# A decoder's last expert layer: its first 16 tiles among the last four groups, with a table of their own

## The chip, the cores and the metric

The kernel runs on one core of a Trainium2 chip. The time is device microseconds (us) of one execution, the median of several. The engines are PE (TensorE: matmuls and transposes), DVE (VectorE), ACT (ScalarE), POOL (GpSimd) and SP (SyncE, which only issues DMAs). Each runs its own instruction stream strictly in order and waits for others through semaphores.

## The reference

A two-layer decoder with residual layer norms works on 64 x 64 = 4096 tokens of width 128. Layer 0: retention-like attention, cross attention, and eight experts that are computed for all tokens. Layer 1: attention, cross attention (its context is `ctx_2048`), and a block that the change concerns, attention followed by a mixture of experts:

```python
x1 = _layernorm(x + attn_out, g1, be1)
gate_probs = softmax(x1 @ Wg + bg)
topk_p, topk_i = top_k(gate_probs, 2)                    # 2 of 8 experts
topk_p = topk_p / sum(topk_p)
comb = sum(one_hot(topk_i, 8) * topk_p[..., None], axis=-2)
h = gelu(einsum('bsd,edf->bsef', x1, W1) + b1)           # 128 -> 512
y = einsum('bsef,efd->bsed', h, W2) + b2                 # 512 -> 128
return _layernorm(x1 + einsum('bse,bsed->bsd', comb, y), g2, be2)
```

Then comes the outer residual layer norm. Each token needs two of the eight experts, so there are 8192 pairs of a token and an expert.

## The kernel before

**Groups and slots.** The tokens are cut into 16 groups of 256. There are four sets of buffers, the slots s = 0 to 3, and four passes n; group 4n + s of a pass runs in slot s. In the first half (streams 0 to 15) each group goes through layer 0, and in the second (streams 16 to 31, so "group 28" to "group 31" are the last four) through layer 1 as far as the ranks of its rows. A stream is a generator that yields the name of its next step; `in_turn` (L413) runs an engine through a table of pairs (stream, count), `ORDERS`. These tables are written out for each engine and stage (sp1, pe1, act1, dve1, pool1 for the groups; sp3 to dve3 for the expert tiles; sp4 to act4 for the end), and they alone set which step stands behind which.

**The end of a group.** PE's last steps are: reductions of the attention ("fr", "frt"), output projection ("fo"), transposes of x1 ("t4"), gate logits ("g", four matmuls at L2166, before which ACT copies x1 at L1213) and ranks ("rk", L2171). ACT takes the exponential of the gate's two best. DVE takes sum and layer norm ("n3"), the choice of two ("g"), weights ("gb", which also adds the group's counts to `base`, L1423) and the rows' places ("rk", last at L1707). Each of a group's 512 pairs gets a row in `rows_x`, a DRAM table of 38912 rows of 132 floats (x1, token row, other expert, two gates), in which expert e owns the rows from 4096 e on. POOL writes them with four indirect scatters of 128 rows each (step "sc", L1081). SP stores the group's states ("fq.1": x_last, L845; "x1": x1_last, L848), which the end of the kernel loads again.

**Blank rows.** An expert's last tile is not full, so `rows_x` must be cleared before. After `blank` is set (`s_blank`), SP issues four DMAs of 5016 KB each (L818) right after the first loads, ahead of all the rest of sp1. POOL waits for them in `fetch` (L1009) before its first gather, at the start of the second half. In the first half SP also stores x_mid (step "gb", L796) and expert outputs ("ye3", "ye7") and loads the next pass's transposed inputs ("u7", L760).

**Expert tiles.** A tile is 256 rows of one expert; 39 tiles are enough for any routing. After all 16 groups, PE counts the rows of each expert (L2181), waits for the places of the last pass in all slots, and DVE makes from the counts a table of 39 pairs, row address and weight address (L1720 to L1732). SP meanwhile waits for each slot's places and stores, issues the first weights (L868, `Q<-in_wm`), waits for the scatters of all slots, and issues the first row loads (L862, `XW<-rows_x`). The first two rounds (`FIXED = 2`, eight tiles) have addresses that are known beforehand, since tile k of them is the first of expert k; the others take theirs from the table. Then the tiles run in rounds over the four slots, tile 4j + s in slot s:

- PE: two transposes of the rows ("tx", L1808), eight matmuls up in four steps ("up", L2196), sixteen down ("dn", L2203)
- ACT: copy of the transposed rows (L1323), four Gelu (L1327)
- DVE: the gates and addresses of the rows ("tp", L1740 to L1748), add of the bias ("ty", L1753; the weights of a slot are loaded again only after it) and two multiplications with the gates (L1756)
- POOL: two indirect scatters into `y_rows` ("sc", L1091)

At the end all results are loaded, summed on PE, normed and stored.

## Time and profile before

| | |
|---|---|
| median of 3 runs | 1558.77 us (1558.26 to 1558.95) |
| the profiled execution | 1557.2 us, of which the span is 1555.4 us |
| mean granted clock of PE | 0.965 of full |
| busy: PE, DVE, ACT, POOL | 88%, 71%, 60%, 43% of the span |
| groups 30 and 31 end (last places matmul to its end) | about 1312 us |
| expert tiles on PE | 1322 to 1481 us |
| after them, to the end | 74 us |

Times in the trace are us from the start of the span. The page gives the span in 40 slices of 38.9 us, each digit being the busy share in tenths. A row of the timeline reads: start, duration, engine, line, operation with output and inputs, and in brackets the idle time before it and what released it. In the waits, a row gives engine and line, what it waited for, and total, number and longest. SPq rows are a DMA from its issue until it landed.

### The profile page before, as it was taken

The numbers are of one execution on the slowest core, as the hardware profiler recorded it, in microseconds if no ns is written. First come the engines' busy times: TensorE is split into PE (matmuls) and PEld (weight loads), VectorE is DVE, ScalarE is ACT, GpSimd is POOL, SyncE is SP. The second block draws the span as 40 slices with busy tenths as digits, with TensorE's granted clock in tenths as the row PEclk, the third lists the DMA queues.
The fourth block names the chain that finished last, engine by engine and source line by source line (L and its number), as shares of the span: only waits on it lengthen the run. The fifth ranks groups of instructions, "written<-read, shape, count | busy, mean of one in ns | idle before, by whom it ended". The sixth has DMA issues, their size and how long they took to land.

```text
span 1555.4 us, 47442 instructions
## 1 busy us (share of the span) xinstructions
PE 1366.5 (88%) x19262; PEld 1123.0 (72%) x19262; DVE 1109.8 (71%) x3476; ACT 935.6 (60%) x2469; POOL 671.9 (43%) x1048
## 2 busy tenths in 40 slices
PE   5899999999988998899998899998899984999951
PEld 4688888888876777676776677776777763888851
DVE  3777787887876758888667887778876775445556
ACT  2555665655544687855878658795568962545412
POOL 5514433533316214655234753337441344254455
PEclk8899999999999999999999999999999996999985
DMA  9952122121022000110000110011100003676851
GB/s 333 384 174 83 35 83 92 53 65 66 15 74 74 9 12 18 44 30 29 10 21 25 36 43 10 14 32 37 29 23 9 13 23 100 208 224 211 237 148 42
DMA packets 112155, 123.21 MB, mean 79 GB/s; under 512 B 21984, under 2 KB 85216, under 8 KB 111680
## 3 DMA queue, kind: packets, MB, share of 16 engines
q1 hardware_dynamic: 105344, 106.53, 21.7%
q0 software_dynamic: 6592, 13.64, 2.8%
q8 instruction: 152, 2.49, 0.7%
q14 instruction: 67, 0.55, 0.1%
HBM read 64.99 MB, written 55.15 MB: 77 GB/s over the span
## 4 chain that ended last, share of the span: by engine, by line
PE 48%; DVE 23%; POOL 8%; ACT 8%; issue 6%; DMA 5%; SPq 2%; DVEq 0%; POOLq 0%; ACTq 0%
PE bank L1949 6%; PE bank L1816 5%; PE bank L1801 3%; PE bank L1828 3%; DMA Q<-in_wm 2%; PE bank L2036 2%; PE bank L2071 2%; PE bank L1997 2%; DVE P L1581 2%; DVE gs L1580 2%; ACT P L1226 2%; PE bank L1993 2%; PE bank L2203 2%; PE bank L2196 2%; POOL rows_x L1081 2%
## 5 line engine op out<-in xcount | busy, mean ns | idle before, releaser
L1816 PE MATMUL bank<-const,P 128*128 128x128 f32 x1152 | 167.9, 280 | 9.9 <-ACT P L1226 4.1
L1816 PEld LDWEIGHTS bank<-const,P 128*128 128x128 f32 x1152 | 129.8, 142 | 39.4 <-ACT P L1226 10.0
L1226 ACT ACTIVATE P<-bank,gs 128x128 f32<-128x128 f32 x512 | 141.3, 393 | 26.4 <-DVE gs L1570 25.9
L1949 PE MATMUL bank<-XT,wb 128*128 128x256 f32 x512 | 140.4, 398 | 7.0 <-ACT PT L1131 3.8
L1036 POOL TENSOR_TENSOR P<-P,gs 128x512 f32<-128x512 f32 x64 | 66.5, 1047 | 157.1 <-DVE gs L1617 156.7
L1234 ACT ACTIVATE PT<-bank 128x512 f32<-128x512 f32 x192 | 108.2, 614 | 28.9 <-PE bank L1816 28.6
L1091 POOL DMA_INDIRECT y_rows<-R,gidx x78 | 74.7, 958 | 92.5 <-DVE R L1756 73.7
L1570 DVE TENSOR_REDUCE gs<-bank 128x4 f32<-128x512 f32 x128 | 82.1, 682 | 39.4 <-PE bank L2071 38.8
L1949 PEld LDWEIGHTS bank<-XT,wb 128*128 128x128 f32 x512 | 89.3, 192 | 22.2 <-ACT PT L1131 7.5
L1580 DVE TENSOR_REDUCE gs<-bank 128x8 f32<-128x512 f32 x128 | 87.1, 681 | 24.5 <-PE bank L2009 12.1
L1198 ACT ACTIVATE P<-bank 128x256 f32<-128x256 f32 x128 | 48.5, 380 | 84.5 <-PE bank L1949 83.8
L1327 ACT ACTIVATE PT<-bank,Q 128x256 f32<-128x256 f32 x156 | 64.8, 475 | 56.5 <-PE bank L2196 55.7
L946 POOL TENSOR_SCALAR rstd<-mv 128x2 f32<-128x2 f32 x80 | 18.1, 226 | 183.1 <-DVE mv L1358 182.3
L1219 ACT ACTIVATE P<-P 128x512 f32<-128x512 f32 x128 | 80.3, 643 | 19.7 <-DVE P L1581 19.3
L1581 DVE TENSOR_TENSOR P<-bank,gs 128x512 f32<-128x512 f32 x128 | 88.5, 691 | 4.4
L1081 POOL DMA_INDIRECT rows_x<-XW,places x64 | 64.4, 1006 | 49.4 <-DVE places L1707 39.3
L2196 PE MATMUL bank<-XT,Q 128*128 128x256 f32 x312 | 77.1, 385 | 4.8 <-DMA Q<-in_wm 4.8
L1828 PEld LDWEIGHTS bank<-wb,P 128*128 128x128 f32 x512 | 73.5, 193 | 9.7 <-DVE P L1511 4.6
L1828 PE MATMUL bank<-wb,P 128*128 128x128 f32 x512 | 78.4, 280 | 2.3 <-DVE P L1511 2.2
L1015 POOL DMA_INDIRECT Q<-y_mid,first_rows x64 | 64.3, 1004 | 29.5 <-DVE first_rows L1556 16.6
L2203 PE MATMUL bank<-Q,PT 128*128 128x128 f32 x624 | 76.1, 275 | 0.0
L2203 PEld LDWEIGHTS bank<-Q,PT 128*128 128x128 f32 x624 | 74.8, 192 | 1.5
(298 smaller groups left out, 3723.3 us busy)
## 6 DMA issues: line engine op xcount, KB each, us to landing
Q<-in_wm SPq DMA_DIRECT2D x39, 578.5 KB, 4.2
rows_x<-blank SPq DMA_DIRECT2D x4, 5016.0 KB, 37.7
y_mid<-PT SPq DMA_DIRECT2D x16, 512.0 KB, 3.1
y_mid<-D SPq DMA_DIRECT2D x16, 512.0 KB, 3.0
XW<-rows_x SPq DMA_DIRECT2D x39, 132.0 KB, 2.5
wb<-in_wb SPq DMA_DIRECT2D x1, 4228.0 KB, 15.0
V<-in_ctxT SPq DMA_DIRECT2D x32, 128.0 KB, 3.4
XT<-in_xT SPq DMA_DIRECT2D x16, 128.0 KB, 2.2
```

The source lines that it names most:

```text
L1081: pool.indirect_dma_start(d["rows_x"][:, :], bass.IndirectOffsetOnAxis(ap=places[:, (n * SLOTS + s) * T + t, k:k + 1], axis=0), XW[s][:, t ...
L1219: act.activation(P[s][:, i, :], P[s][:, i, :], ACT.Exp, scale=scale).then_inc(p.of(s), 1)
L1226: ins = act.activation(P[s][:, i, 128 * g:128 * g + 128], banks[s][i][:, 128 * g:128 * g + 128], ACT.Exp, bias=gs[s][:, 0, 4 * i + g:4 * i ...
L1234: act.activation(dst[:, i, :], banks[s][i][:, :], ACT.Copy).then_inc(pT.of(s), 1)
L1570: dve.tensor_reduce(gs[s][:, 0, 4 * i:4 * i + 4], banks[s][i][:, :].rearrange("p (g m) -> p g m", m=128), AX.X, ALU.min).then_inc(b_s_sub. ...
L1580: st2(dve.tensor_reduce(mx, v, AX.X, most))
L1581: dve.tensor_tensor(P[s][:, i, :].rearrange("p (g m) -> p g m", m=width), v, each(mx, width), ALU.subtract).then_inc(s_sub.of(s), 1)
L1816: last = pe.transpose(tile(banks[s][i], t), tile(P[s][:, i, :], t), ident)
L1828: last = mm(tile(half(s, i + 1), t), tile(P4[s][:, i + 1, :], t), tile(B("down"), e), start=True, stop=True)
L1949: mm(half(s, 2 * (e % 2) + k), tile(B("gu"), 2 * e + k), XT[s][:, :], start=True, stop=True).then_inc(a_up_ps.of(s), 1)
L2196: mm(half(s, c), tile(part(wm[s], WM, "w1"), c), XT[s][:, :], start=True, stop=True).then_inc(m_up_ps.of(s), 1)
L2203: ins = mm(tile(half(s, 0), t), tile(PT4[s][:, c, :], t), tile(part(wm[s], WM, "w2"), c), start=c == 0, stop=c == NC - 1)
```

## The change

- **Early tiles.** The tiles are split into 16 early ones and 23 late ones. The early tiles are full tiles: the table for them is made from the counts of the first 12 groups whose rows are ranked (`COUNTED`, `EARLY_PASSES = 3`), of which at least 16 tiles are complete. They sit in slots by `EARLY_SLOTS`: slot 0 has tiles 0, 1, 2, 4, 6, 9, slot 1 has 3, 5, 7, 10, 13, slot 2 has 8, 11, 14 and slot 3 has 12, 15. Their steps stand in the tables of the groups (sp1, pe1, act1, dve1, pool1), among the steps of groups 28 to 31.
- **Waits of a slot's first tile.** SP waits for the table and the last use of the group's buffers to load weights, and for the group's own stores and scatters of all four passes and the other slots' of three passes to load rows. PE waits for the slot's places.
- **Two tables.** PE takes the count inside "rk" of the 12th and of the 16th group ranked, DVE copies it to `plan`. `early_table` (stream 33) stands in dve1 right behind the end of group 27, `late_table` (stream 50) among the early tiles. The first four late tiles wait for the second table and all scatters; all 39 tiles take their addresses from the table.
- **Clearing.** The four DMAs at the start go. After each of the 16 x_mid stores ("gb") SP clears one of 16 parts, about 1.25 MB each; the first gather waits for all 16.
- **Orders.** All tables are new. In those of the groups common steps shift by at most 14 positions; in the last stage group 8 stands ahead of 5.

Near the end PE's order now reads (group in brackets, t0 is tile 0; several "fr", "fn", "fs" and "fp" steps left out): [29] rk, [31] fp1, [30] fr1, **[t0] tx**, [31] fp1, [30] frt, [30] fo, [31] fr1, **[t0] up, up.1, up.2**, [31] fn, **[t0] up.3**, [31] frt, fo, [30] t4, **[t3] tx**, [30] g, **[t0] dn, [t3] up, up.1**, [31] t4, [30] rk, **[t3] up.2, up.3**, [31] g, **[t1] tx, [t3] dn, [t5] tx, [t1] up, up.1, up.2**, [31] rk, **[t1] up.3, [t5] up**, and then only tiles, in the order 0, 3, 1, 5, 8, 2, 12, 7, 11, 4, 15, 10, 6, 14, 13, 9. ACT: [31] fp1, **[t0] tx**, [30] frt, [31] fp1.1, fr1, **[t0] up**, [31] frt, **[t0] up.1 to up.3**, [30] t4, **[t3] tx**, [30] g, **[t3] up, up.1**, [31] t4, **[t3] up.2, up.3**, [31] g. DVE: [31] n3, **[t0] ty**, [30] gb, rk, **[t3] tp**, [31] g, **[t3] ty**, [31] gb, rk. SP: [31] out1, fq.1, [29] fq.1, x1, [28] fq.1, x1, **[t0] tw, tx, [t3] tw, tx**, [30] fq.1, x1, **[t8] tw, [t1] tx, tw**, [31] x1, **[t5] tx, tw, [t8] tx**. POOL: [28] sc, [29] sc, fo and n3 of [30] and [31], **[t0] sc**, [30] sc, **[t3] sc**, [31] sc, **[t1] sc**.

```diff
-FIXED = 2
-ROUNDS = [(TILES - s + SLOTS - 1) // SLOTS for s in range(SLOTS)]
+EARLY_PASSES = 3
+EARLY_SLOTS = (0, 0, 0, 1, 0, 1, 0, 1, 2, 0, 1, 2, 3, 1, 2, 3)
+EARLY = len(EARLY_SLOTS)
+LATE = TILES - EARLY
+TILE_SLOTS = EARLY_SLOTS + tuple(k % SLOTS for k in range(LATE))
+ROUNDS = [TILE_SLOTS.count(s) for s in range(SLOTS)]
+COUNTED = (EARLY_PASSES * SLOTS, EARLY_PASSES * SLOTS + SLOTS)
+TURNS = [(i, TILE_SLOTS[:i].count(s), s) for i, s in enumerate(TILE_SLOTS)]
...
+            def clear_rows(k):
+                fours = XROWS // 128 // 4
+                lo, hi = fours * k // groups, fours * (k + 1) // groups
+                sp.dma_start(d["rows_x"].rearrange("(p a r) d -> p a (r d)", p=128, r=4)[:, lo:hi, :],
+                             over(blank[:, :], hi - lo)).then_inc(s_clear, 16)
...
+                if n == 0 and s == 0:
+                    sp.wait_ge(s_blank, 1)
+                clear_rows(n * SLOTS + s)
...
-            for at in range(0, each_row, BLANK):
-                sp.dma_start(d["rows_x"].rearrange("(p a r) d -> p a (r d)", p=128, r=4)[:, at // 4:(at + BLANK) // 4, :],
-                             over(blank[:, :], BLANK // 4)).then_inc(s_clear, 16)
...
-            for s in range(SLOTS):
-                sp.wait_ge(b_g_done.of(s), b_g_done.at(passes - 1, s))
-                sp.wait_ge(kept[s], 32 * passes)
-                load_weights(0, s)
-            for s in range(SLOTS):
-                sp.wait_ge(scattered[s], 16 * 2 * T * passes)
-            for s in range(SLOTS):
-                load_rows(0, s)
...
-            def tile(j, s):
-                yield "tx"
-                if j == FIXED:
-                    sp.wait_ge(s_table, 1)
+            def tile(i, j, s):
                 if j:
+                    yield "tx"
+                    if i - EARLY in range(SLOTS):
+                        sp.wait_ge(s_table, 2)
+                        for other in range(SLOTS):
+                            sp.wait_ge(scattered[other], 16 * 2 * T * passes)
                     sp.wait_ge(m_x_ps.of(s), m_x_ps.at(j - 1, s))
                     sp.wait_ge(m_row.of(s), m_row.at(j - 1, s))
-                    load_rows(j, s)
-                yield "tw"
-                if j:
+                    load_rows(i, s)
+                    yield "tw"
                     sp.wait_ge(m_y.of(s), m_y.at(j - 1, s))
-                    load_weights(j, s)
-                if 1 <= j <= 2:
-                    load_last_x1(j - 1, s)
-                    load_last_x(j - 1, s)
-
-            in_turn(sp, ORDERS["sp3"], [tile(j, s) for j in range(ROUNDS[0]) for s in range(SLOTS) if j < ROUNDS[s]])
+                    load_weights(i, s)
+                else:
+                    yield "tw"
+                    sp.wait_ge(s_table, 1)
+                    sp.wait_ge(b_s_ps.of(s), b_s_ps.at(passes - 1, s, use=7))
+                    load_weights(i, s)
+                    yield "tx"
+                    sp.wait_ge(kept[s], 32 * passes)
+                    for other in range(SLOTS):
+                        sp.wait_ge(scattered[other], 16 * 2 * T * EARLY_PASSES)
+                    sp.wait_ge(scattered[s], 16 * 2 * T * passes)
+                    load_rows(i, s)
+                if i >= EARLY and (i - EARLY) // SLOTS < 2:
+                    load_last_x1((i - EARLY) // SLOTS, s)
+                    load_last_x((i - EARLY) // SLOTS, s)
...
+                if emitted[n, s] + 1 in COUNTED:
+                    k = COUNTED.index(emitted[n, s] + 1)
+                    dve.tensor_copy(plan[0:1, NE * k:NE * k + NE], banks[s][1][0:1, T * NE:T * NE + NE]).then_inc(s_count, 1)
...
-            dve.tensor_copy(prim[:, :], prim[:, :]).then_inc(s_count, 1)
-            dve.wait_ge(s_count, 2)
...
+            def tiles_of(found, inner, at, n):
+
+                mid(dve.tensor_tensor(grid(S(at, 64), NE), grid(one(C("upto")), NE), over(found, NE), ALU.mult))
+                mid(dve.tensor_reduce(S(at + 64, NE), grid(S(at, 64), NE), AX.X, ALU.add))
+                mid(dve.tensor_tensor(grid(S(at + 72, 7 * n), 7), each(one(C("tile"))[:, 0:n], 7), over(S(at + 64, 7), n), ALU.is_ge))
+                mid(dve.tensor_tensor(grid(S(at + 240, 7 * n), 7), grid(S(at + 72, 7 * n), 7), over(inner, n), ALU.mult))
+                dve.tensor_reduce(S(at + 410, n), grid(S(at + 240, 7 * n), 7), AX.X, ALU.add)
+                mid(dve.tensor_reduce(S(at + 440, n), grid(S(at + 72, 7 * n), 7), AX.X, ALU.add))
+
+            def put_table(i0, at, n):
+                mid(dve.scalar_tensor_tensor(S(at + 500, n), S(at + 440, n), CAP / NT, S(at + 470, n), ALU.mult, ALU.add))
+                dve.tensor_scalar(grid(S(at + 530, 2 * n), 2)[:, :, 0], S(at + 500, n), float(NT), None, ALU.mult)
+                mid(dve.tensor_scalar(grid(S(at + 530, 2 * n), 2)[:, :, 1], S(at + 440, n), 128.0, None, ALU.mult))
+                dve.tensor_copy(table[:, i0:i0 + n, :], grid(S(at + 530, 2 * n), 2)).then_inc(s_table, 1)
+
+            full, done, step, left, inner = S(160, NE), S(168, NE), S(176, 7), S(184, NE), S(192, 7)
+
+            def early_table():
+                yield "pl"
+                at = 220
+                dve.wait_ge(s_count, 1)
+                mid(dve.tensor_tensor(grid(S(16, 128), 16), each(S(0, NE), 16), over(one(C("steps")), NE), ALU.is_ge))
+                mid(dve.tensor_reduce(full, grid(S(16, 128), 16), AX.X, ALU.add))
+                tiles_of(full, full[:, 0:7], at, EARLY)
+                mid(dve.scalar_tensor_tensor(S(at + 470, EARLY), S(at + 410, EARLY), -1.0, one(C("tile"))[:, 0:EARLY], ALU.mult, ALU.add))
+                put_table(0, at, EARLY)
+                yield "pl.1"
+                mid(dve.tensor_scalar(S(144, NE), S(at + 64, NE), float(EARLY), None, ALU.min))
+                dve.tensor_copy(done[:, 0:1], S(144, 1))
+                mid(dve.tensor_tensor(done[:, 1:NE], S(145, 7), S(144, 7), ALU.subtract))
+                mid(dve.tensor_tensor(step, done[:, 1:NE], done[:, 0:7], ALU.subtract))
+
+            def late_table():
+                yield "pl"
+                at = 220
+                dve.wait_ge(s_count, 2)
+                mid(dve.tensor_tensor(grid(S(16, 128), 16), each(S(NE, NE), 16), over(one(C("below")), NE), ALU.is_gt))
+                mid(dve.tensor_reduce(left, grid(S(16, 128), 16), AX.X, ALU.add))
+                mid(dve.tensor_tensor(left, left, done, ALU.subtract))
+                mid(dve.tensor_tensor(inner, step, left[:, 0:7], ALU.subtract))
+                tiles_of(left, inner, at, LATE)
+                mid(dve.tensor_tensor(S(at + 470, LATE), S(at + 410, LATE), one(C("tile"))[:, 0:LATE], ALU.add))
+                mid(dve.tensor_scalar(S(at + 470, LATE), S(at + 470, LATE), done[:, 0:1], None, ALU.add))
+                put_table(EARLY, at, LATE)
...
+                if emitted[n, s] + 1 in COUNTED:
+                    mm(banks[s][1][0:1, T * NE:T * NE + NE], C("full")[:, 0:1], base[:, emitted[n, s] + 1, 0, :], start=True, stop=True)
...
-            pe.wait_ge(s_count, 1)
-            for s in range(SLOTS):
-                pe.wait_ge(b_g_done.of(s), b_g_done.at(passes - 1, s))
-            mm(banks[0][0][0:1, 0:NE], C("full")[:, 0:1], base[:, groups, 0, :], start=True, stop=True).then_inc(s_count, 1)
-            pe.wait_ge(s_table, 1)
-
-            def tile_of(j, s):
+            def tile_of(i, j, s):
                 yield "tx"
                 pe.wait_ge(tile_x[s], 16 * (j + 1))
                 if j:
                     pe.wait_ge(m_y.of(s), m_y.at(j - 1, s))
+                else:
+                    pe.wait_ge(b_g_done.of(s), b_g_done.at(passes - 1, s))
```

## Rows read from the trace of the kernel before

**Rows 1.** Page, part 2: PE busy tenths and moved GB/s in 40 slices.

```profile
PE   5899999999988998899998899998899984999951
...
GB/s 333 384 174 83 35 83 92 53 65 66 15 74 74 9 12 18 44 30 29 10 21 25 36 43 10 14 32 37 29 23 9 13 23 100 208 224 211 237 148 42
```

**Rows 2.** Stretches: length, busy (count) PE PEld DVE ACT POOL, clock, DMA, GB/s; page part 5.

```profile
1295.00:1313.30 18.30, 6.73 (x30) 5.04 (x28) 10.54 (x62) 1.56 (x5) 8.71 (x12) 0.60 0.39 134
...
1313.30:1322.30 9.00, 0.20 (x2) 0.13 (x3) 3.81 (x16) 0.00 (x0) 3.83 (x4) 0.50 0.45 131
...
1322.30:1481.30 159.00, 150.54 (x1014) 137.76 (x1014) 76.75 (x426) 76.96 (x196) 71.13 (x75) 0.99 0.73 220
...
L2196 PE MATMUL bank<-XT,Q 128*128 128x256 f32 x312 | 77.1, 385 | 4.8 <-DMA Q<-in_wm 4.8
```

**Rows 3.** Timeline, end of last groups: start, us, engine, line, operation [idle before <-releaser].

```profile
1300.78 1.02 PE L2166 MATMUL bank<-wb,XT 128*128 128x8 f32 x4 [0.47 <-ACT XT L1213]
...
1307.47 1.08 POOL L1081 DMA_INDIRECT rows_x<-XW,places  x1 [4.08 <-DVE places L1707]
...
1311.64 0.58 PE L2171 MATMUL bank<-gs,const 128*128 128x16 f32 x2 [3.32 <-DVE base L1423]
...
1322.31 0.66 PE L1808 MATMUL bank<-const,XW 128*128 128x128 f32 x2 [8.45 <-DMA XW<-rows_x]
```

**Rows 4.** Waits from 1322 to 1482: us in total, times, longest.

```profile
PE bank L1808 <- DMA XW<-rows_x: 12.0, 7, 8.5
...
PE bank L2196 <- DMA Q<-in_wm: 4.8, 6, 1.2
...
DVE small L1740 <- DMA Q<-in_wm: 24.5, 13, 6.4
```

**Rows 5.** Timeline of POOL: first scatter of group 28 and of group 29.

```profile
1255.58 1.08 POOL L1081 DMA_INDIRECT rows_x<-XW,places  x1 [9.97 <-DVE places L1707]
...
1286.84 1.08 POOL L1081 DMA_INDIRECT rows_x<-XW,places  x1 [10.04 <-DVE places L1707]
```

**Rows 6.** DMA issues (times, KB, median us to landing), and landing of line 868.

```profile
XW<-rows_x SPq DMA_DIRECT2D x39, 132.0 KB, 2.5
...
rows_x<-XW,places POOLq DMA_INDIRECT x64, 2.4
...
DMA to landing us min/median/max: 3.5/4.2/6.6
```

**Rows 7.** Timeline of ACT: first Gelu of the tile stage.

```profile
1324.43 0.66 ACT L1323 ACTIVATE XT<-bank 128x256 f32<-128x256 f32 x2 [1.05 <-PE bank L1808]
...
1325.11 1.28 ACT L1327 ACT_TABLE_LOAD   x1
```

**Rows 8.** Timeline of DVE (table), and line 1753 over the run: ns min/median/max.

```profile
1313.89 0.28 DVE L1720 TENSOR_TENSOR plan<-bank,const 1x128 f32<-1x128 f32 x1 [0.31 <-PE bank L2181]
...
1317.56 0.24 DVE L1732 CAST table<-plan 1x78 int32<-1x78 f32 x1
...
L1753 DVE TENSOR_TENSOR R<-bank,Q x39: 423/424/426, 1330.6 to 1481.3; 128x256 f32<-128x256 f32 x39
```

**Rows 9.** Timeline of PE, the same operations at other times.

```profile
1267.27 0.61 PE L2166 MATMUL bank<-wb,XT 128*128 128x8 f32 x4
...
1324.19 1.83 PE L2196 MATMUL bank<-XT,Q 128*128 128x256 f32 x4
...
1330.45 1.03 PE L2196 MATMUL bank<-XT,Q 128*128 128x256 f32 x4
```

**Rows 10.** Stretches, as rows 2.

```profile
1120.00:1160.00 40.00, 38.29 (x582) 30.04 (x581) 32.76 (x91) 26.89 (x68) 17.34 (x29) 1.00 0.09 25
```

**Rows 11.** Last blank DMA, a PE wait between 40 and 460, first gather.

```profile
50.09 14.14 SPq L818 DMA_DIRECT2D rows_x<-blank  x1
...
PE bank L1841 <- DMA XT<-in_xT: 2.1, 1, 2.1
...
464.31 1.22 POOL L1015 DMA_INDIRECT Q<-y_mid,first_rows  x1 [16.64 <-DVE first_rows L1556]
```

More of the change, by code:

```diff
@@ L62 @@
                       ("cos", 64), ("sin", 64), ("par", 2), ("side", 2), ("quad", 4), ("iota", 8),
-                      ("ones", 8), ("full", 128), ("before", 128), ("eoff", 8), ("steps", 16), ("upto", 64),
+                      ("ones", 8), ("full", 128), ("before", 128), ("eoff", 8), ("steps", 16), ("below", 16), ("upto", 64),
                       ("tile", TILES), ("rowbase", 32), ("spare", TILES * T))
@@ L1757, in tile @@
                 ins.then_inc(m_gated.of(s), 1)
-            in_turn(dve, ORDERS["dve3"], [tile(j, s) for j in range(ROUNDS[0]) for s in range(SLOTS) if j < ROUNDS[s]])
+            in_turn(dve, ORDERS["dve1"], [whole(n, s, first, second) for n in range(passes) for s in range(SLOTS)]
+                    + [whole(n, s, first2, second2) for n in range(passes) for s in range(SLOTS)]
+                    + [between(), early_table()] + [tile(*turn) for turn in TURNS[:EARLY]] + [late_table()])
+            in_turn(dve, ORDERS["dve3"], [tile(*turn) for turn in TURNS[EARLY:]])
             def finish(n, s):
```

118 lines of the change are left out of this document (53 added, 65 removed), and 446 rows, old and new, of tables (ORDERS, act1, act3, dve1).

## The prediction

> **What bounds the kernel now.** I read the page's slices first [rows 1]: of the 40 slices, TensorE is busy eight tenths or more in all but the first (5), the 34th (4) and the last two (5 and 1). So time is lost where its row dips, and the dip in the 34th is where the change works. The table of stretches [rows 2] prices it. From 1295.0 to 1313.3, while groups 30 and 31 (the last two) end, PE is busy 6.73 of 18.3 us; from there to 1322.3 it is busy 0.20 of 9.0; then all 39 expert tiles run in 159.0 us with PE busy 150.54. The timeline [rows 3] says why. Gate logits of group 30 are at 1300.78, its scatter starts at 1307.47, the place matmuls of group 31 are at 1311.64: short steps handed between PE, ACT and DVE with nothing else queued. Then PE counts the rows, DVE makes the table, POOL scatters, SP loads tile rows, and PE gets them at 1322.31. In the waits [rows 4] this load is the one long one (8.5 us); the tile stage has otherwise waits of at most 1.2 us, so it is bound by PE.
>
> **The unit.** One tile is 150.54 / 39 = 3.86 us of PE. By the page its eight up matmuls, four steps of two, take 77.1 / 39 = 1.98 [rows 2], 0.5 a step ("up"); of the rest I give 0.4 to the transposes ("tx") and 1.5 to the sixteen down matmuls ("dn").
>
> **Part 1: sixteen tiles enter before the old end.** Read from the decoded orders, few of them truly run among the groups: between "fr1" of group 30 and "rk" of group 31 PE now does tile 0 and tile 3 whole, tx of tiles 1 and 5 and three of the four up steps of tile 1: 2 x 3.86 + 2 x 0.4 + 3 x 0.5 = 10.0 us. The PE holes of 1295 to 1313 (11.6 us) are about that large. Are the rows there? Tile 0 (slot 0) needs group 28's scatter, which began at 1255.58 and, four issues of 1.3 us and 2.4 us of landing later, is in by 1264; tile 3 (slot 1) needs group 29's, begun at 1286.84, in by 1294.3, plus a 2.5 us load: 1297 [rows 5, 6]. Both are in time. SP's new order puts "fq.1" of group 31 ahead of the final stores of groups 29 and 28; in the trace such a store waits for its data anyway, until about 1273, which is still 15 us early.
>
> The other fourteen early tiles (all but 0 and 3) follow group 31's "rk" with no wait for the count, the table or all scatters; those are due only for tile 16, some 50 us later. So the 9.0 us hole and the rest of it goes. What is late next is slot 2's row load (scatter of group 30, issued from 1307.47 [rows 3], now behind tile 0's y scatter of 2 x 1.26 us on POOL): landed about 1317, loaded 1319.5, while PE has tiles 1 and 5 to do until about 1319. Slot 3's load lands about 1326, PE comes to it at 1327. Neither costs over 1 us.
>
> **Part 2: what the insertion delays.** The chain of groups 30 and 31 sets where the rest starts.
> - ACT must switch between Gelu (tiles) and Exp (the gates, "g"). The order has Gelu, Exp for group 30, Gelu, Exp for group 31, Gelu: four switches more than before. A load took 1.28 us [rows 7]. Two stand in the chain: +2.6 us. The Trainium skill (ScalarE: Activation LUTs, What ACT_TABLE_LOAD costs) speaks against this mixing: it states 1283 ns for the load plus some 1380 ns of drain at every switch. The trace agrees with the first number and shows no drain: the copy before ended within 0.03 us of the load. By the page the chain would be 2.8 us longer, and the forecast 1549.
> - DVE takes "ty" of tiles 0 and 3 ahead of "gb" of group 30 and of group 31: 0.42 us for the add [rows 8] and about as much for the two gate steps, +1.8 us if both are waited for.
> - Against it, a PE that has work keeps its clock. The granted clock was 0.60 of full in the mean from 1295 to 1313 and 0.50, the 1.2 GHz level, from there to 1322, while PE idled; the logits took 1.02 us there and 0.61 at 1267.27, before the fall [rows 2, 3, 9]. I take -1.5 us over both groups.
> Net +3: between -1.5 (all hidden) and +7 (all in series, plus up steps ahead of the logits). So rk of group 31 ends at 1315.6 instead of 1312.6.
>
> **Part 3: the rest of the tiles.** Remaining PE work: 150.5 - 10.0 - 1.3 (the cold start: the first four up matmuls took 1.83 us, four later ones 1.03, and so the transposes and the steps after them, some 0.5 more [rows 9]) = 139.2 us. Idle of the tile stage was 159.0 - 150.54 = 8.5 us. It grows where a slot is used again too soon: weights wait for "ty", so y add 0.42, issue 0.35, landing 4.2 [rows 6, 8] and about 0.5 for signals, 5.5 us, must lie under other tiles' PE work. The old order left three tiles (11.6 us) between two of one slot. The new one has four places with one tile between (3.9 us: stall 1.6 each) and about six with two (7.7 us: covered unless the landing is the slowest, 6.6). Two of the four are inside the group chain where PE waits anyway. I add 4 us, bounds 0 and 12. End of tile work: 1315.6 + 139.2 + 12.5 = 1467.3 against 1481.3: **14.0 us earlier**.
>
> **Part 4: table and count.** The old table, 13 DVE steps from 1313.89 to 1317.80, lay inside the hole that goes. Now the early table, some 20 small DVE steps, stands after group 27's ranks, near 1127. At the price of the old one, 13 steps in 3.9 us [rows 8], it is 4 to 6 us of DVE in one piece, where DVE is busy 32.76 of 40 us and PE 38.29 [rows 10]. Four groups are in flight and cover most; I take 1 us of PE, bounds 0 and 5. The late table is under tiles where DVE is busy half the time [rows 2]: nothing; without that cover it would be 5 us. The two added count matmuls replace one, before the place matmuls of two groups: nothing.
>
> **Part 5: clearing.** The same 20 MB go out in 16 pieces of 1.25 MB, each behind an x_mid store, instead of four at 18 us that hold SP's queue until 64 us and move 333 and 384 GB/s in the first two slices, 174 in the third [rows 1, 11]. What waited behind them on SP were loads for the next round; PE waited for such a load once in the first stage, 2.1 us [rows 11]. Gain at most 2.1. Cost: at 384 GB/s a piece is 3.3 us of all engines, ahead of y stores and xT loads on SP, 16 times, 0 to 4 us in all. At the hand-over near 451 to 464 the last piece lands by about 460, before first_rows is ready at 464.31 [rows 11]; with that cover gone each late us would count. I take 0, bounds -2 and +4.
>
> **Part 6: new orders elsewhere.** Positions shift by at most 14 among some 1200 to 2150 steps; in the tail, 74.1 us from 1481.3 to the end, the reduction of group 8 moves ahead of 5. No row prices them: 0, bounds -4 and +4, some two times the 1.7 us that PE idles in a 40 us window [rows 10].
>
> **Sum.** The profiled execution has a span of 1555.4 us and took 1557.2, 1.8 outside the span and 1.6 under the median 1558.77. Change: -14.0 + 1 = -13.0, taken from the median: **1546 us**.
>
> **Rivals.**
> - *Only the hole goes.* If inserted tiles push groups 30 and 31 back by as much as they take, the gain is 1312.6 to 1322.3, 9.7, plus 1.3 cold start, less 4 and 1: 6 us, 1553. For it: PE, ACT and DVE run strictly in order and there are four table loads. Against it: PE's holes there are real waits.
> - *Everything fits.* No delay of the chain, no reuse stalls: 3 + 4 more, and 1 or 2 from the clearing: 1538.
> - *Nothing left.* The price of reuse or of the phase orders eats it: 1556 to 1562.
> - *Slower: slots starve.* Slot 0 has six of the sixteen tiles, slot 1 five. SP's single queue holds a weight load behind another slot's row load, which waits for PE. If each of the ten short reuses costs 4 us, 40 instead of 4: +36 - 13.0, 1582; it decides from 2 us each (20 against 4 + 13.0). For it: landings up to 6.6 us [rows 6], and DVE waited for them 13 times, 24.5 us in all, with four slots in turn [rows 4]. Against it: those PE waits were at most 1.2 us [rows 4].
>
> **How the numbers follow.** Forecast 1540 to 1551: 0.52. Everything fits: 0.12, a third of it under 1536. Only the hole: 0.17. Nothing left, within 0.2% (3.1 us, about what a measurement can tell from no change): 0.10. Slower: 0.09. Faster by over 0.2% is the first three: 0.81. The range 1536 to 1557 leaves out 0.04 below and about 0.15 above.
>
> **What would show it.** Right: PE busy some 9 or 10 us more between 1290 and 1316; no PE wait of 8.5 us for rows_x; a clock near 1.0 through 1300 to 1340; five or so ACT table loads near 1300; the last dn near 1467 and a tail of the same 74 us. Wrong: the stretch of groups 30 and 31 longer by as much as its tiles take; PE waits for Q<-in_wm of over 2 us each; PE idle near 1130 or at 451 to 480 grown by several us, which would put the time above 1551.

## The result, and the profile after

The changed kernel takes 1550.84 us (median; 1542.93 to 1556.62), the kernel before in the same comparison 1558.16 (1554.7 to 1559.53): a ratio of 0.9953, 95% interval 0.9937 to 0.9968, or 7.3 us faster. The forecast was 1546, range 1536 to 1557. The number lies in the range, and the sign is right. The mechanism behind it is not: the experiments below show that merging tiles and groups, as this change does it, brings nothing that can be measured, and that the two new sets of orders alone reach the same time, which I had put at 0. That the number held is luck.

The profiled execution of the changed kernel took 1556.62 us, the longest of its executions, with a span of 1554.8. So its total says little, but its stages can be compared with those of other traces. From its page, part 2 (busy tenths of PE, its clock and GB/s moved, 40 slices), which answers to [rows 1]:

```profile
PE   6799999999989998899998899998999987898871
...
PEclk9999999999999999999999999999999999999986
...
GB/s 255 10 160 153 73 134 136 115 136 94 53 160 54 16 9 25 40 26 28 10 28 18 47 33 9 14 32 35 31 23 9 9 25 107 189 227 222 200 186 42
```

The dip of the 34th slice is gone (4 before, 7 now); so are the 333 and 384 GB/s of blank rows in the first two slices, now spread over the first twelve. But slices 35 to 38 read 8988 where they read 9999 before. What was filled was opened again.

To see where time goes, I cut the span at events that both kernels have: the first gather on POOL (start of the second half), the end of the place matmuls of groups 19, 27 and 31, the end of the last down matmul, and the end. The table of stretches at these cuts, first of before, then of after (length; busy and count of PE, PEld, DVE, ACT, POOL; clock, DMA share, GB/s):

```profile
0.00:464.30 464.30, 423.92 (x4733) 364.13 (x4734) 346.30 (x1071) 256.76 (x677) 179.58 (x272) 0.97 0.36 122
464.30:718.90 254.60, 231.82 (x3850) 182.16 (x3849) 191.60 (x519) 169.88 (x444) 119.29 (x188) 0.99 0.11 31
718.90:1125.60 406.70, 374.18 (x6679) 291.96 (x6679) 317.53 (x878) 290.42 (x771) 190.38 (x303) 1.00 0.09 26
1125.60:1312.60 187.00, 159.24 (x2892) 125.21 (x2891) 131.68 (x373) 127.69 (x349) 67.23 (x107) 0.95 0.09 28
1312.60:1481.30 168.70, 150.79 (x1017) 137.89 (x1016) 81.10 (x444) 76.96 (x196) 74.96 (x79) 0.96 0.71 214
1481.30:1555.40 74.10, 26.57 (x96) 21.63 (x96) 41.53 (x195) 13.92 (x32) 40.42 (x100) 0.69 0.31 90
```

```profile
0.00:460.90 460.90, 422.19 (x4733) 362.23 (x4734) 348.27 (x1070) 255.40 (x678) 179.78 (x273) 0.99 0.35 123
460.90:714.10 253.20, 232.55 (x3849) 182.12 (x3847) 193.43 (x519) 168.97 (x443) 119.72 (x188) 0.98 0.11 31
714.10:1129.40 415.30, 379.77 (x6682) 296.91 (x6682) 322.74 (x878) 291.26 (x771) 190.36 (x303) 0.99 0.09 25
1129.40:1322.20 192.80, 173.17 (x2958) 135.80 (x2958) 139.22 (x412) 139.16 (x368) 71.14 (x111) 0.96 0.12 36
1322.20:1485.10 162.90, 145.04 (x953) 130.02 (x952) 75.89 (x425) 70.95 (x182) 71.75 (x76) 0.98 0.70 212
1485.10:1554.80 69.70, 24.70 (x96) 20.02 (x96) 41.23 (x195) 14.04 (x32) 40.59 (x100) 0.73 0.32 95
```

Three things are to be seen. The fifth row: 953 matmul instructions instead of 1017 stand behind group 31's ranks, so about 2.4 tiles were done before, as meant; yet the stretch is only 5.8 us shorter, and the one before it 5.8 us longer. In these two traces the merging nets zero. The third row: groups 20 to 27, in which no tile runs, are 8.6 us longer with the same instructions. The first and last row: 3.4 and 4.4 us shorter. I had put the three together at 0, plus or minus 4.

The same cuts in every trace of this study (us; the last column is the ratio to the kernel before of the same comparison, with its interval):

| kernel | to first gather | to 19 | 20 to 27 | 28 to 31 | tiles | end | ratio |
|---|---|---|---|---|---|---|---|
| before | 464.3 | 254.6 | 406.7 | 187.0 | 168.7 | 74.1 | 1 |
| before, again (b0) | 464.0 | 254.1 | 406.6 | 188.4 | 169.7 | 73.5 | |
| after | 460.9 | 253.2 | 415.3 | 192.8 | 162.9 | 69.7 | 0.9953 (0.9937 to 0.9968) |
| a0 (after, again) | 457.4 | 253.6 | 412.5 | 193.5 | 164.1 | 69.7 | 0.9961 (0.9945 to 0.9976) |
| clear_at_start | 459.0 | 252.8 | 414.0 | 191.1 | 163.0 | 69.8 | 0.9929 (0.9913 to 0.9946) |
| tiles_behind | 458.2 | 254.5 | 412.1 | 185.4 | 175.0 | 69.8 | 1.0001 (0.9986 to 1.0016) |
| old_tail | 461.4 | 254.0 | 412.6 | 190.3 | 164.7 | 73.5 | 0.9986 (0.9969 to 1.0004) |
| round_robin | 457.1 | 253.0 | 414.7 | 190.4 | 155.2 | 71.5 | 0.994 (0.9923 to 0.9957) |
| old_second_half | 459.1 | 255.1 | 405.5 | 199.8 | 163.9 | 69.0 | 0.995 (0.9933 to 0.9968) |
| exp_tiles | 458.2 | 254.6 | 416.3 | 192.9 | 165.8 | 70.0 | 0.9973 (0.9958 to 0.9987) |
| ty_between | 457.4 | 253.1 | 413.0 | 189.8 | 163.4 | 69.8 | 0.9957 (0.994 to 0.9973) |
| middle_old | 456.1 | 254.0 | 406.2 | 193.7 | 164.3 | 69.1 | 0.9907 (0.9889 to 0.9926) |
| no_merge | 462.1 | 254.8 | 412.3 | 185.1 | 172.2 | 70.6 | 0.9951 (0.9933 to 0.9968) |
| best | 457.7 | 253.0 | 406.5 | 193.3 | 152.9 | 70.7 | 0.9891 (0.9871 to 0.991) |

A trace is one execution, the ratio many. I read a stage only where several traces agree, and take the verdict from the ratio. A stage's length also moves with the granted clock of its execution, so for the tiles I read the idle time of PE (length less busy), with the mean clock beside it. It is 17.9 us in before (0.96), 17.9 in after (0.98), 18.6 in a0 (0.98), and 17.2 to 20.8 in all eight traces that have the changed kernel's slots with tiles among the groups; 14.0 in round_robin (1.00) and 9.6 in best (0.98).

### The profile page after: what moved, and what is told of

Same layout as the page of the kernel before. It is cut to its first block, busy times and chain, and to the rows that moved or that the text cites. A ratio compares the mean times of both kernels' runs of the same rounds, so it can differ in the third digit from the quotient of the medians.

```text
span 1554.8 us, 47583 instructions
## 1 busy us (share of the span) xinstructions
PE 1377.4 (89%) x19264; PEld 1127.1 (72%) x19264; DVE 1120.8 (72%) x3497; ACT 939.8 (60%) x2473; POOL 673.3 (43%) x1048
## 4 chain that ended last, share of the span: by engine, by line
PE 44%; DVE 25%; POOL 10%; ACT 8%; issue 6%; DMA 5%; SPq 2%; DVEq 0%; POOLq 0%; ACTq 0%
PE bank L1856 5%; PE bank L1989 4%; PE bank L2111 2%; PE bank L1868 2%; PE bank L2076 2%; PE bank L1841 2%; PE bank L2037 2%; PE bank L2238 2%; PE bank L2033 2%; DVE gs L1588 2%; DVE P L1589 2%; POOL rows_x L1088 2%; PE bank L2231 2%; DMA Q<-in_wm 2%; POOL rstd L954 2%
## 5 line engine op out<-in xcount | busy, mean ns | idle before, releaser
L1856 PE MATMUL bank<-const,P 128*128 128x128 f32 x1152 | 169.6, 283 | 10.9 <-ACT P L1226 4.0
L1241 ACT ACTIVATE PT<-bank 128x512 f32<-128x512 f32 x192 | 109.3, 619 | 33.5 <-PE bank L1856 33.4
L953 POOL TENSOR_SCALAR rstd<-mv 128x2 f32<-128x2 f32 x80 | 18.2, 228 | 191.6 <-DVE mv L1365 190.4
L1226 ACT ACTIVATE P<-P 128x512 f32<-128x512 f32 x128 | 80.1, 642 | 18.6 <-DVE P L1589 18.0
L1088 POOL DMA_INDIRECT rows_x<-XW,places x64 | 64.2, 1003 | 31.9 <-DVE places L1718 20.8
```

Of the source, the lines that this page charges most:

```text
L1088: pool.indirect_dma_start(d["rows_x"][:, :], bass.IndirectOffsetOnAxis(ap=places[:, (n * SLOTS + s) * T + t, k:k + 1], axis=0), XW[s][:, t ...
L1226: act.activation(P[s][:, i, :], P[s][:, i, :], ACT.Exp, scale=scale).then_inc(p.of(s), 1)
L1241: act.activation(dst[:, i, :], banks[s][i][:, :], ACT.Copy).then_inc(pT.of(s), 1)
L1856: last = pe.transpose(tile(banks[s][i], t), tile(P[s][:, i, :], t), ident)
```

## Is the spread the kernel's own? a0 and b0

```diff
 (a0: the changed kernel; b0: the kernel before; no edit)
```

> The changed kernel as it is, in the same call as the next three, so that they can be compared with it. Its executions so far lay between 1543 and 1557 us. If that spread belongs to the kernel, these lie in the same band, median near 1550, and execution time falls as the mean granted clock rises (0.970 at 1554, 0.979 at 1541). If it came from the chip of the first job, they lie within 3 us of each other.

> The kernel before once more, for a second trace. If the stages differ between the kernels and not between executions, it shows first gather near 464, 406 to 408 us from the ranks of group 19 to 27, 187 to 31, 169 to the last down matmul and 74 to the end, each within 1.5 us.

a0: 1552.59 us (1549.08 to 1554.69), ratio 0.9961 against before. b0: 1558.27 us, and each stage within 1.5 us of the first trace, as expected. So 6 to 10 us more in groups 20 to 27 and 2 to 5 us less at the end are the kernel's and not chance: all traces with the respective order show them. To the first gather all traces with the new order are shorter too, by 2 to 8 us, but only 2 to 3 us of it can be put down to the order: where the mean clock of that stage is as low as in before (0.97), in old_tail and no_merge, it takes 461.4 and 462.1 us against 464.0 and 464.3. The changed kernel spreads by 14 us in the first comparison and by 6 in this; in both the time falls as the granted clock rises (correlation -0.83 and -0.77).

## What the orders alone bring: no_merge

```diff
 (the kernel before; FIXED, table, count, clearing and the tile stage untouched)
-ORDERS sp1, pool1, act1, dve1, pe1: of before
+ORDERS sp1, pool1, act1, dve1, pe1: of after, steps of tiles and tables left out
-ORDERS sp4, pool4, act4, dve4, pe4: of before
+ORDERS sp4, pool4, act4, dve4, pe4: of after
```

> The kernel before with nothing of the change but its orders: of the groups (tile steps left out) and of the last stage. Tiles, table, count and clearing are as before. My forecast put 14 us of gain into the merging of tiles and groups and nothing into the orders: then this equals the kernel before. The stage table says the reverse: first gather 5 us sooner, end 4 us shorter, groups 20 to 27 7 us longer, groups 28 to 31 2 us shorter, the tile stage as before (169 us), together 1553 to 1555, which is nearly all of the change's gain.

1552.53 us (1548.18 to 1559.07), ratio 0.9951 (0.9933 to 0.9968). The whole change has 0.9953 and 0.9961. So all that was done to the tiles, the two tables and the clearing, adds nothing that can be measured (each interval reaches some 2.5 us either way) to what two sets of orders bring. The reason of the forecast is refuted though its number held. The trace of this run is of its slowest execution (1559.07), so its stages don't add up to the gain; the stage differences that several traces share (about -2 to -5 to the first gather, +7, -2, -4 at the end) sum to -1 to -4 us; the rest of the 7.6 isn't located.

## Does merging bring what it was to bring? tiles_behind and round_robin

**tiles_behind** puts the early tiles behind the groups again, in their new sequence of slots:

```diff
+def behind(order, first, keep=()):
+    pairs = list(zip(order[0::2], order[1::2]))
+    late = [p for p in pairs if p[0] >= first and p[0] not in keep]
+    return sum([p for p in pairs if p not in late] + late, ())
+for _name, _first, _keep in (("sp1", 32, (32, 35)), ("pool1", 32, ()), ("act1", 32, ()), ("dve1", 34, ()), ("pe1", 33, ())):
+    ORDERS[_name] = behind(ORDERS[_name], _first, _keep)
```

> The changed kernel with every early tile step of PE, ACT, DVE and POOL behind the last step of group 31 (SP keeps the loads of the first two slots where they are). If the inserted tiles fill true holes of groups 30 and 31 and delay them by 3 us, as forecast, 10 us of PE work now follow instead: 6 to 8 us slower than the changed kernel. If only the hole between the stages brings the gain (the inserted tiles push the groups back by what they take), it is the same within 2 us, and group 31's places are ranked near 1312 instead of 1322.

1558.15 us, ratio 1.0001: 5.6 us slower than a0, near the 6 to 8 of the first theory and far from "the same". The stages show both halves of the forecast's Part 1 and 2: without the inserted tiles groups 28 to 31 take 185.4 us (185.1 in no_merge) instead of 190.3 to 193.5, so 9 to 10 us of tile work cost the groups 5 to 8. That is more than the 3 I took. And the tile stage, with no hole for count and table any more, takes 175.0 us, more than the 168.7 with that hole; 2.0 us of this are idle time (19.9 against 17.9), 4.3 are busy time of the same work. PE's waits from 1310.2 to 1485.2 (line, releaser: us in total, times, longest):

```profile
PE bank L2241 <- DMA Q<-in_wm: 10.3, 13, 1.8
PE bank L1858 <- DMA XW<-rows_x: 6.3, 6, 2.2
```

Before it was 4.8 for the weights and 12.0 for rows, of which 8.5 was the hole [rows 4]. Without it, 8.3 us of waiting for loads have become 16.6. In the changed kernel itself, from 1285 to 1482:

```profile
PE bank L2231 <- DMA Q<-in_wm: 10.4, 11, 2.0
PE bank L1848 <- DMA XW<-rows_x: 6.0, 5, 2.8
```

None is longer than 2.8 us, so no single stall stands out on a timeline. The hole has gone and many small waits have taken its place. The suspect is the slots, six of 16 tiles in slot 0 and five in slot 1. Counted in the tables of PE, 3 of the 35 times that a slot comes again it does so with one other tile between, and 12 times with two; in the kernel before it is 0 and 7, with three or more between in the rest.

**round_robin** tests that. Slots in turn give 2 and 7 such places; the order of the tiles and the place of the second table change with them:

```diff
-EARLY_SLOTS = (0, 0, 0, 1, 0, 1, 0, 1, 2, 0, 1, 2, 3, 1, 2, 3)
+EARLY_SLOTS = (0, 1) + (0, 1, 2, 3) * 3 + (0, 1)
-TILE_SLOTS = EARLY_SLOTS + tuple(k % SLOTS for k in range(LATE))
+TILE_SLOTS = EARLY_SLOTS + tuple((k + 2) % SLOTS for k in range(LATE))
-ORDERS: tiles 0, 3, 1, 5 (slots 0, 1, 0, 1) among the groups, then 8, 2, 12, 7, 11, 4, ...
+ORDERS: tiles 0, 1, 2, 3 (slots 0, 1, 0, 1) at the same places, then 4, 5, ... in the relative order of before
```

> The changed kernel with two tiles instead of tile 0 and tile 3 at their places among the groups, and all later tiles in turn over the four slots in the relative order of the kernel before. In the first comparison the stretch from the last ranks to the last down matmul holds 163 to 165 us, of which some 22 are idle, 16 of them waits for weights and rows. If slots that come again too soon cause that, the stretch falls to 150 to 155 us and the time by 8 to 12 us against the changed kernel. If something else fills it (the stores of the groups, scatters, the clock), it stays within 3 us.

1548.06 us (1543.71 to 1553.52), ratio 0.994. The stretch of the tiles is 155.2 us against 162.9 and 164.1, at the edge of what was expected. In the table of stretches:

```profile
1315.20:1470.40 155.20, 141.22 (x953) 127.75 (x952) 77.17 (x425) 71.12 (x183) 70.17 (x74) 1.00 0.72 220
```

Of these 7.7 us, 3.9 are the slots': idle time of PE is 14.0 us where the changed kernel has 17.9. The other 3.8 are busy time, 141.2 instead of 145.0 for the same 953 instructions, with a clock of 1.00 instead of 0.98, and so belong to this execution, the fastest of its kernel (1543.71). Of the whole time 2 to 4.5 us show against the changed kernel, less than the 8 to 12 expected and with intervals that overlap (0.9923 to 0.9957, and 0.9945 to 0.9976 for a0); 1.7 us go at the end, where PE waited 10.3 us instead of 8.6 for the results to be loaded. That the slots cause idle time is shown by PE's waits for weights and rows (11.8 us here, 15.3 to 19.2 in the traces with the changed slots); the whole time alone doesn't settle it.

## The insertion among the groups: exp_tiles and ty_between

**exp_tiles** has the exponential in place of Gelu in the tiles, so it leaves that layer's function out and ACT needs no other table:

```diff
-                    act.activation(PT4[s][:, c, :], half(s, c), ACT.Gelu, bias=...)
+                    act.activation(PT4[s][:, c, :], half(s, c), ACT.Exp, bias=...)
```

> The changed kernel with exponential instead of Gelu in the last layer's tiles, which leaves the function of that layer out, so that ACT needs no other table among the groups. If the four added loads of 1.28 us lie in the chain of the last two groups as forecast (two of them), the ranks of group 31 come 2 to 5 us sooner after those of group 29, and the time is 2 to 4 us lower. If PE has other work meanwhile, the time is the same within 1.5 us.

1553.35 us, ratio 0.9973; no table load between 1290 and 1345, and 34.2 us from the ranks of group 29 to those of 31, the same as in the changed kernel (34.2 and 36.2). The mean clock of that stretch was 0.90 in exp_tiles and in the first trace of the changed kernel, both 34.2 us, so these two can be compared: the loads cost nothing that shows. The timeline of ACT in the changed kernel shows why:

```profile
1307.02 0.38 ACT L1327 ACTIVATE XT<-bank 128x256 f32<-128x256 f32 x1
1307.42 1.28 ACT L1322 ACT_TABLE_LOAD   x1
1309.12 0.20 ACT L1322 ACTIVATE small<-small 128x2 f32<-128x2 f32 x1 [0.42 <-DVE small L1396]
...
1315.24 1.28 ACT L1322 ACT_TABLE_LOAD   x1
1316.76 0.20 ACT L1322 ACTIVATE small<-small 128x2 f32<-128x2 f32 x1 [0.24 <-DVE small L1396]
```

Both loads for the gates' exponential are done while DVE still chooses the two experts: the exponential waits 0.42 and 0.24 us for DVE after them. In exp_tiles the first of these waits is 1.72 us, about the load and the wait together. The copy ended 0.02 us before the load began. The Trainium skill (ScalarE: Activation LUTs, What ACT_TABLE_LOAD costs) counts a drain of some 1380 ns beside the load; no switch here shows it. The ratio's interval (0.9958 to 0.9987) overlaps that of a0 (0.9945 to 0.9976), so this is no difference, and in any case not the 2 to 4 us of gain.

**ty_between** takes away the other suspect. The timeline of DVE in the changed kernel, with the steps of group 31's gate, tile 3's bias add ("ty") and group 31's "gb":

```profile
1316.33 0.39 DVE L1395 CAST gs<-gidx 128x4 f32<-128x4 uint32 x1
1316.41 0.31 DVE L1396 TENSOR_TENSOR small<-gs 128x2 f32<-128x2 f32 x1
1318.99 0.42 DVE L1790 TENSOR_TENSOR R<-bank,Q 128x256 f32<-128x256 f32 x1 [2.27 <-PE bank L2238]
1319.85 0.16 DVE L1419 TENSOR_SCALAR XW<-const 128x2 f32<-128x2 f32 x1
```

The exponential was ready at 1316.96; DVE held "gb" back until 1319.85, for the down matmuls of tile 3 and its add: 2.9 us, of which I had counted 0.9 as work and nothing as a wait for PE. But most of that wait is the clock. PE's down matmuls of tile 0 and of tile 3 in the same trace:

```profile
1307.64 2.03 PE L2238 MATMUL bank<-Q,PT 128*128 128x128 f32 x16
...
1315.27 3.68 PE L2238 MATMUL bank<-Q,PT 128*128 128x128 f32 x16 [0.31 <-ACT PT L1331]
```

From 1315.4 to 1318.8 the granted clock was 0.50. Where the lower level missed tile 3 (old_tail, exp_tiles), its sixteen took 2.05 us and DVE waited 0.65 us; where it fell on them (after, a0, clear_at_start, round_robin), 3.56 to 3.74 us, and DVE waited 2.16 to 2.80.

```diff
 (dve1 only)
-[31] n3, [t0] ty, [30] gb, rk, [t3] tp, [31] g, [t3] ty, [31] gb, rk
+[31] n3, [30] gb, [t0] ty, [30] rk, [t3] tp, [31] g, [31] gb, [t3] ty, [31] rk
```

> The changed kernel, but on DVE the bias add and gate steps of tile 0 and of tile 3 stand behind gb of groups 30 and 31 instead of ahead of it (ahead of rk). In a trace of the changed order DVE sat idle 2.7 us before the add of tile 3 until PE's sixteen down matmuls ended, with gb of group 31 ready behind it. If this wait is what delays the last two groups, their ranks come 2 to 4 us sooner after those of group 29 (36.2 and 34.2 us in two traces) and the time is 2 to 4 us lower. If the ranks wait for PE's own work ahead of them, the same within 1.5 us.

Its trace has 33.1 us from the ranks of group 29 to those of 31. That is no proof of a gain: with the chain unedited clear_at_start has 33.4 and old_tail 32.5 us (mean clock 0.95), round_robin and after 34.0 and 34.2 (0.90, as in ty_between), a0 36.2 (0.81). At the same clock it is 1 us less. The time is 1552.69 us, ratio 0.9957, not to be told from 0.9961. A miss, and PE's timeline of the changed kernel shows why. Between tile 3's down matmuls and group 31's ranks stand steps of tiles 5 and 1:

```profile
1319.57 0.41 PE L1848 MATMUL bank<-const,XW 128*128 128x128 f32 x2 [0.61 <-DVE R L1790]
1319.81 1.46 PE L2231 MATMUL bank<-XT,Q 128*128 128x256 f32 x6
1321.47 0.20 PE L2212 MATMUL bank<-base,const 128*1 128x8 f32 x2 [0.20 <-DVE base L1431]
```

The first of them itself waits for tile 3's add (0.61 us). PE came to the ranks only 0.20 us before DVE's "gb" was ready (0.21 in a0, round_robin and clear_at_start). The expectation's second branch holds: the ranks wait for PE's own work ahead of them. From the ranks of group 29 to those of 31 PE is busy 26.57 us in after and 15.68 in before; 10.9 us more of work lengthen the stretch by 5.1.

## The orders of the groups and of the end

**old_second_half** and **middle_old** go back to the old order of the groups (PE, ACT, DVE, POOL), the first from the end of group 19 on, the second only to the end of group 27. At these cuts old and new order have done exactly the same steps.

```diff
 (middle_old; counts are steps)
-pe1 1152 to 1860, act1 811 to 1295, dve1 667 to 1057, pool1 221 to 389: order of after
+pe1 1152 to 1860, act1 811 to 1295, dve1 667 to 1057, pool1 221 to 389: order of before
```

> The changed kernel with the order of the groups as before from the end of group 19 on (PE, ACT, DVE, POOL; SP's stays new), tile steps behind the same group steps. From the ranks of group 19 to those of group 27 the trace of before took 406.7 us and five traces with the new order 412.1 to 415.3. If the new order of these groups costs that, 4 to 6 us faster than the changed kernel. My term for it was 0, plus or minus 4; if the difference is chance of single executions, the same within 2 us.

> The changed kernel with the order of the kernel before on PE, ACT, DVE and POOL from the end of group 19 to the end of group 27 only, and the new order up to there and from there. That stretch took 405.5 us with the old order in the kernel with the old second half, 406.7 and 406.6 in two traces of before, and 412 to 416 with the new. If it is the order, 6 to 8 us faster than the changed kernel. If the stretch only hands the gain on to the next (199.8 us in the kernel with the old second half against 193), the same within 2 us.

old_second_half: 1550.45 us, ratio 0.995, no gain, though groups 20 to 27 take 405.5 us as they should. Groups 28 to 31 take 199.8 instead of 193. There tiles and groups meet in an order made for other neighbours; PE's waits from 1119.7 to 1319.5 begin with

```profile
PE bank L2242 <- DVE base L1460: 3.5, 2, 3.3
```

where the changed order has 1.0: PE stands at group 30's ranks, for DVE waited 3.10 us for tile 0's down matmuls before that group's choice could go on. In this trace too the lower level lay on them (0.50 from 1296.1 to 1302.9; they took 3.58 us), so how much is the order's isn't told apart. middle_old keeps the new order where tiles are, and is 1545.34 us, ratio 0.9907 (0.9889 to 0.9926): 7 to 8 us faster than the changed kernel by the ratios, the middle 406.2 us. So the new order of groups 20 to 27, positions shifted by at most 14, costs some 7 us, and in the changed kernel it eats half of what the rest gains. PE idles 30.0 to 32.5 us in this stage in the five traces with the old order and 35.5 to 36.3 in the nine with the new. By its waits (before and after), those for DVE's V grow from 1.7 to 4.7 us and for DVE's X from 2.0 to 4.2, those for ACT's P shrink from 7.4 to 5.1. Which shifted step does it was not tried.

**old_tail** has the tables sp4 to pe4 of before:

```diff
-    pe4=(0, 1, 1, 1, 2, 1, 3, 1, 4, 1, 8, 1, 5, 1, 6, 1, 10, 1, 7, 1, 9, 1, 13, 1, 11, 1, 15, 1, 14, 1, 12, 1))
+    pe4=(0, 1, 1, 1, 2, 1, 3, 1, 4, 1, 5, 1, 6, 1, 7, 1, 8, 1, 9, 1, 10, 1, 11, 1, 12, 1, 13, 1, 14, 1, 15, 1))
```

> The changed kernel with the orders of the last stage (after the tiles) as before. My term was 0. The traces show 69.7 us from the last tile's end to the end of the span against 74.1: if the new order brings that, this kernel is 4 us slower than the changed one; if it is the clock or chance, the same within 1.5 us.

1557.48 us, ratio 0.9986: 4.9 us slower than a0, and 73.5 us from the last down matmul to the end against 69.7. The intervals overlap slightly (0.9969 to 1.0004, and 0.9945 to 0.9976), but the end is 73.5 to 74.1 us in all three traces with the old order and 69.0 to 71.5 in the eleven with the new. So the new order of the last stage is worth about 4 us. In the waits of PE in this stage, a0 and then old_tail:

```profile
PE bank L2253 <- DVE mv L1365: 4.9, 3, 2.8
```

```profile
PE bank L2263 <- DVE mv L1375: 6.9, 1, 6.9
```

The sum of group 8 (third pass) needs DVE's statistics of group 0; the wait of 6.9 us in one piece (6.8 in before) is cut to 4.9 in three. That is half of the 4 us; where the rest lies was not looked at.

## The clearing: clear_at_start

```diff
-                if n == 0 and s == 0:
-                    sp.wait_ge(s_blank, 1)
-                clear_rows(n * SLOTS + s)
...
+            sp.wait_ge(s_blank, 1)
+            for k in range(0, groups, 4):
+                clear_rows(k)
```

(with four groups' parts in one DMA, and the first gather waiting for four)

> The changed kernel, but blank rows are cleared by four DMAs at the start as before. My term for the clearing was 0: then this equals the changed kernel within 2 us. The rival from the two traces: group 16 was ranked 6.3 us sooner after the change and group 23 3.8 us sooner, and this comes from the clearing; then this kernel is 3 to 6 us slower than the changed one, and its first gather is at about 464, not 461.

1548.74 us (1544.76 to 1551.65), ratio 0.9929, in the same comparison as a0's 0.9961: some 4 us faster, with intervals that just touch. The rival, slower by 3 to 6, is refuted: the first gather is at 459.0, so the early start of the second half doesn't come from the clearing. That splitting costs 4 us isn't shown with the same right. No stage of the trace holds them (the stages differ from a0's by less than 2.5 us each, in both directions), so the cause stays open.

## The best of both: best

Round robin, the middle in old order, the adds behind "gb", clearing at the start:

> Round robin of the tiles, the old order of the groups from the end of group 19 to the end of group 27, the bias adds of the first two tiles behind gb, and clearing by four DMAs at the start, all in one. Measured alone against the changed kernel (1551 to 1552.6 us): round robin -3.5, the middle -6 to -7, the start -3, the adds 0. If they act in different stages, they add up: 1538 to 1541 us. If they only pass a shared slack on to one another, it is no better than the best of them alone, 1545 us.

1537.44 us (1534.32 to 1540.66), before in the same comparison 1554.5: ratio 0.9891 (0.9871 to 0.991). It beats both kernels. That the edits add up in full isn't shown: the kernel before took 1554.5 us in this comparison and 1558.2 to 1559.2 in the others, so the 1537.44 is flattered. The ratios of the single edits would add up to 0.9854 (from a0's 0.9961) or 0.987 (from 0.9953), and the gain to 0.9891 is two thirds to three quarters of that. Nor is it told from middle_old alone (0.9889 to 0.9926). Its tiles:

```profile
1310.50:1463.40 152.90, 143.35 (x953) 129.41 (x952) 77.53 (x425) 70.80 (x181) 71.27 (x76) 0.98 0.73 223
```

PE idles 9.6 us in the tiles (17.9 in after, 18.1 in middle_old, 14.0 in round_robin with the same slots). Its waits from 1300 to 1465:

```profile
PE bank L1875 <- DMA XW<-rows_x: 5.0, 6, 2.1
PE bank L2258 <- DMA Q<-in_wm: 4.4, 6, 1.5
```

From the ranks of group 27 to the last down matmul it takes 346.2 us (193.3 + 152.9), round_robin 345.6, and before 355.7 and 358.1. So in these stages merging with the slots in turn is 10 to 12 us shorter, against 0 in the changed kernel (355.7 and 357.6). In the whole time that isn't confirmed: round_robin has 0.994 (0.9923 to 0.9957) and no_merge, without any merging, 0.9951 (0.9933 to 0.9968).

## Why the prediction was right, and where it was wrong

- **Part 1, what enters early**: 10.0 us forecast; 1014 - 953 = 61 matmul instructions, 61 / 1014 x 150.54 = 9.1 us. Right: PE was busy 19.9 us between 1290 and 1316 where it had been 10.9, and the rows were in time.
- **Part 2, the delay of the groups**: +3 forecast, bounds -1.5 and +7. 29.1 us from the ranks of group 29 to those of 31 (in both traces of before) became 32.5 to 36.2: +3.4 to +7, from near the forecast to the upper bound (37.2 in middle_old, at a clock of 0.82). The terms were the wrong ones. The table loads, which I put at 2.6, cost nothing; DVE's steps and its wait for tile 3's down matmuls are covered, since PE comes to the ranks 0.2 us before DVE is ready. What lengthens the stretch is PE's own tile work ahead of the ranks. The clock, which was to give 1.5 back, gives it only where no stretch at the lower level falls into this stretch: 0.91 in the mean from 1295 to 1313.3 instead of 0.60, but 3.4 us at 0.50 right behind, from 1315.4.
- **Part 3, the tiles behind group 31**: this is the step that failed. 139.2 us of work and 12.5 idle, 151.7 us; measured 162.9: 145.0 busy and 17.9 idle, and the last down matmul at 1485.1 instead of 1467. The idle time is the reuse of slots, for which I took 4 us on top of 8.5, with 12 as the bound; it was 9.4 (8.7 to 12.3 in the eight traces). I had also miscounted: not four places with one tile between and about six with two, but 3 and 12, and the 12 were taken as covered. That loads of one slot also queue behind another's on SP, which I left out of the sum, may add to it; it was not tried by itself. Of the 5.8 us more of busy time 0.9 is work that had not been done before; some 3.4, half of 6.8, lie with two stretches of 3.4 us at the lower level (from 1359.7 and 1455.3), where the kernel before had none from 1326 to its last down matmul (round_robin, with none, is busy 141.2). The rest, about 1.5 us, is open. With slots in turn the stretch has 155.2 and 152.9 us: my number was that of another kernel.
- **The rival "slots starve"** had the right mechanism and too high a price: 4 to 8 us of idle time in the tiles (17.9 against 14.0 and 9.6) instead of 36.
- **Part 4, early table**: +1, bounds 0 and 5. From the ranks of group 27 to 28 before took 128.8 us, old_second_half with the table in the same order 130.8: about 2. Inside the bounds.
- **Part 5, clearing**: 0, bounds -2 and +4. Undone, the time fell by some 4, which makes it +4, at the upper bound, and not located.
- **Part 6, orders elsewhere**: 0, bounds -4 and +4 for all together. Measured by stage: 2 to 8 us less to the first gather (2 to 3 at the same clock), 6 to 10 more in groups 20 to 27, 2 to 3 less in groups 28 to 31 (185.1 and 185.4), 4 less at the end; in sum 0.9951 of the time by no_merge, -7.6 us, outside my bounds. Single terms are as large as the bound I gave to the sum. I took "positions shift by at most 14" for small; it is not.
- **The sum** was -13.0 = -14.0 + 1 and came out as -7.3: 0 or so of the -14, and about -7 of a term that stood at 0. Right by two errors of opposite sign, which is luck.

## To carry to other kernels

When a change regenerates an order written out by hand, measure the orders alone first: here they carried all of the gain that can be measured and, in groups 20 to 27, a loss of the same size, and the described feature carried none. A stage bound by one engine has its wait time in many short pieces; sum them by releaser, and when work is moved forward, keep each buffer's distance between uses (here four slots in turn) or the pieces grow by what the move gains: here 17.9 us idle before and after. A step of another stream placed ahead of a chain's step brings with it the wait for its input; before you charge either to the chain, look how long the engine that takes over had been idle (here 0.20 us). And before you read a difference between two single traces, compare their clock stage by stage.

## What was not expected of the hardware

PE's granted clock fell to its lower level (0.50, 1.2 GHz) in single stretches of 3.4 us within busy stages, not at the same places in every execution (among others, in after near 650, 1005, 1039, 1121 and 1360, in a0 near 590, 857, 1133 and 1355), though some places come again in several traces (near 590, 647 and 797). They stand behind stretches with gaps: in the 6.8 us before each of these five in after PE was busy 3.9 to 5.0 us, where its mean in groups 20 to 27 is 91%. One such stretch on a chain's matmuls costs what two executions of the same kernel then differ by: 3.68 us instead of 2.05 for tile 3's sixteen. Execution times follow: in the twelve of the changed kernel the mean clock ran from 0.970 (1554.6 and 1555.9 us) to 0.979 (1542.9), about 12 us for each 0.01, more than the change itself; in the kernel before, 52 executions, 6 us for each 0.01. A single execution of each kernel would have said "no change" (1556.6 against 1557.2).
